# Four weight matrices split once and kept on chip, and eight products in place of nine for each projected chunk

## The reference

```
# layer 0 (layer 1 has the same shape, without the semantic term, and text = first 77 tokens)
q       = heads(x @ W_q)                           # 320 x 320 projection
k_t,v_t = heads(text @ W_k), heads(text @ W_v)     # text = all but the last 4 tokens
probs   = softmax(q @ k_t.T * scale)
qsem    = l2norm(probs @ text)
fused   = q @ k_ip.T * scale + 0.5 * qsem @ l2norm(ip).T
ip_out  = (softmax(fused) * mask) @ v_ip
out     = (probs @ v_t + ip_out) @ W_out + b_out + x   # 320 x 320 projection
```

## Time and profile before

| | |
|---|---|
| median of three runs | 3471.9 us (3469.57 to 3473.32) |
| the profiled execution | 3471.23 us, its span 3469.4 us |
| PE busy | 3351.1 us, 97% of the span |
| DVE busy | 2052.6 us, 59% |
| ACT busy | 1848.9 us, 53% |
| POOL busy | 1095.4 us, 32% |
| granted TensorE clock, mean | 0.990 |

### The profile page before, as it was taken

One profiled execution on the slowest core, in us unless ns is written; L12 is line 12 of the kernel. 1 busy time (PEld: TensorE's weight loads), 2 busy tenths in 40 slices (PEclk: granted clock), 3 DMA queues, 4 the chain that ended last, 5 costly groups with the idle time before them and its releaser, 6 DMA issues.

```text
span 3469.4 us, 65897 instructions
## 1 busy us (share of the span) xinstructions
PE 3351.1 (97%) x24832; PEld 2909.0 (84%) x24832; DVE 2052.6 (59%) x5573; ACT 1848.9 (53%) x4030; POOL 1095.4 (32%) x932
## 2 busy tenths in 40 slices
PE   6999999999999999999999999999999999999868
PEld 4888978887888888888888888888888898889755
DVE  4444455556555565665666556665666656556677
ACT  2333334556555555555655556555655556565757
POOL 2111010234332333233333332333423322222457
PEclk8999999999999999999999999999999999999989
DMA  6433932233358333243356423333336522222232
GB/s 186 112 74 65 106 87 71 71 94 79 89 81 76 94 76 84 78 106 83 96 77 75 93 72 83 81 81 96 99 69 83 68 60 57 61 49 58 52 84 56
DMA packets 659087, 282.78 MB, mean 82 GB/s; under 512 B 481010, under 2 KB 609730, under 8 KB 658772
## 3 DMA queue, kind: packets, MB, share of 16 engines
q1 hardware_dynamic: 658772, 278.57, 38.5%
HBM read 199.44 MB, written 79.04 MB: 80 GB/s over the span
## 4 chain that ended last, share of the span: by engine, by line
PE 87%; DVE 6%; ACT 2%; issue 2%; POOL 1%; DMA 1%; SPq 1%; POOLq 0%; DVEq 0%; ACTq 0%
PE acc L1109 9%; PE acc L1102 9%; PE acc L1105 8%; PE acc L1104 8%; PE acc L1110 8%; PE acc L1103 7%; PE score L1153 4%; PE score L1069 4%; PE spare L1153 4%; PE score L1071 3%; PE av L1140 3%; PE av L1144 3%; PE spare L1192 2%; PE score L1192 2%; PE score L1241 2%
## 5 line engine op out<-in xcount | busy, mean ns | idle before, releaser
L1316 ACT ACTIVATE prob<-score 128x512 f32<-128x512 f32 x1219 | 729.2, 598 | 1205.8 <-PE score L1071 1200.6
L1720 POOL TENSOR_TENSOR prob_lo<-prob,prob_hi 128x512 fp32r<-128x512 f32 x624 | 814.9, 1310 | 1502.1 <-ACT prob_hi L1319 1501.5
L1102 PE MATMUL acc<-tok_v,prob_hi 128*128 128x300 f32 x2240 | 908.8, 406 | 0.9 <-issue 0.9
L1104 PE MATMUL acc<-tok_lo,prob_hi 128*128 128x256 f32 (+1 forms) x2560 | 755.9, 295 | 0.0
L1109 PE MATMUL acc<-tok_v,prob_lo 128*128 128x278 f32 (+1 forms) x2560 | 746.0, 291 | 1.0 <-DVE prob_lo L1424 1.0
L1319 ACT ACTIVATE prob_hi<-score 128x512 fp32r<-128x512 f32 x1219 | 726.1, 596 | 0.0
L1105 PE MATMUL acc<-tok_lo,prob_hi 128*128 128x256 f32 (+1 forms) x2560 | 719.3, 281 | 0.0
L1110 PE MATMUL acc<-tok_v,prob_lo 128*128 128x256 f32 (+1 forms) x2560 | 717.9, 280 | 0.0
L1103 PE MATMUL acc<-tok_v,prob_hi 128*128 128x256 f32 x2240 | 627.7, 280 | 0.0
L1105 PEld LDWEIGHTS acc<-tok_lo,prob_hi 128*128 128x128 f32 (+1 forms) x2560 | 483.8, 189 | 7.2 <-issue 1.8
L1104 PEld LDWEIGHTS acc<-tok_lo,prob_hi 128*128 128x128 f32 (+1 forms) x2560 | 484.5, 189 | 3.6 <-issue 1.9
(11 more groups left out here) (333 smaller groups left out, 5147.6 us busy)
## 6 DMA issues: line engine op xcount, KB each, us to landing
k_ring<-k_scr SPq DMA_DIRECT2D x160, 384.0 KB
tok_v<-v_scr SPq DMA_DIRECT2D x158, 176.0 KB, 3.4
v_ring<-v_scr SPq DMA_DIRECT2D x160, 148.5 KB, 3.4
ctx_t<-in_ctxT SPq DMA_DIRECT2D x16, 1024.0 KB, 8.6
q_ring<-q_scr SPq DMA_DIRECT2D x160, 96.0 KB
v_scr<-v_stage SPq DMA_DIRECT2D x32, 440.0 KB, 2.7
v_scr<-v_stage SPq DMA_DIRECT2D x36, 330.0 KB, 9.5
tok_stage<-in_ctx SPq DMA_DIRECT2D x32, 256.0 KB, 3.1
```

The source lines that it names most:

```text
L1102: e.matmul(out_a[:, 0:SEG + VCOLS], p_hi, tok_v[0:kk, c, seg, v_lo:v_lo + SEG + VCOLS], start=first, stop=False)
L1104: e.matmul(out_a[:, t0:t0 + SEG], p_hi, tok_lo[0:kk, c, seg * SEG:(seg + 1) * SEG], start=False, stop=False)
L1316: e.activation(prob[:, es, :], bank_s[:, :], ACT.Exp, scale=SCALE)
L1720: e.tensor_tensor(prob_lo[:, ps, :], prob[:, es, :], prob_hi.bitcast(F32)[:, ps, :], ALU.subtract).then_inc(s_low[1], 1)
```

## The change

All four matrices are loaded and split once. wq0 is split at the start, and a new job of side "w" with deadline window 12 loads and splits wo0, wq1 and wo1, one after the other. Each has a tile of five blocks of 320 columns: blocks 0, 1 and 4 are the high parts of the three chunks (HI_TILE), 2 and 3 the low parts of chunks 0 and 1 (LO_TILE). The low part of chunk 2 is in the other 64 rows of block 4. The high part of x_in, and of o_t in the closing, stands in both halves of its third chunk, so one product of block 4 with it gives high x high and low x high at once. Products per output chunk are 3 + 3 + 2 = 8.

Each x split has a third ACT copy, and each closing an ACT copy of the high part from one half to the other, which waits for DVE's cast; the products of "finish" on chunk 2 wait for it. The separate staging tiles w_q_raw, w_o_raw and x_raw go: the weights are staged in attn and closing, x in x_res. The low parts of x_in and o_t still have a zeroed half, the other memsets go. Layer-0 jobs have Pause(2) between load and split of x, where they had Pause(1).

The diff, cut to its core:

```diff
+HI_TILE, LO_TILE = (0, 1, 4), (2, 3)
+WEIGHTS = ("wq0", "wo0", "wq1", "wo1")
...
         if UNITS[u][0] == 0:
-            return [w_loads, x_loads, Pause(1), w_split, x_split, Pause(1)] + q
+            return [x_loads, Pause(2), x_split, Pause(1)] + q
         first, second = close(u - B)
-        return [w_loads] + first + [w_split] + second + [lambda: None, x_split, Pause(1)] + q
+        return first + second + [lambda: None, x_split, Pause(1)] + q
+
+    def weights(name):
+
+        def loads():
+            o.add("w_loads", name)
+
+        def split():
+            o.add("w_split", name)
+            put_off(*[("w_split_lo", name, i) for i in range(2)])
+        return [loads, Pause(2), split, drain]
...
-        tasks = [w_split]
+        tasks = [drain]
...
-        return [w_loads] + (fusing if layer == 0 else []) + [Pause(1)], tasks
+        return (fusing if layer == 0 else []) + [Pause(1)], tasks
...
-        if m == 0:
-            o.add("wo_loads", LAST)
...
-        if m == 0:
-            close(LAST)[1][0]()
...
+    add_job([t for name in WEIGHTS[1:] for t in weights(name)], 12, "w")
...
+        w_raw = [attn[:].rearrange("p s h d -> p (s h d)").rearrange("p (k n) -> p k n", k=NM - 1), closing[:, 0:D]]
...
+            def products_of(k):
+
+                if k < NM - 1:
+                    return (HI_TILE[k], 0), (LO_TILE[k], 0), (HI_TILE[k], 1)
+                return (HI_TILE[k], 0), (HI_TILE[k], 1)
...
-                    for i, (wj, xj) in enumerate(((0, 0), (1, 0), (0, 1))):
...
+                    for wj, xj in products_of(k):
+                        mm = e.matmul(bank[bank_of["q", u, m]][0:w, 0:SQ], w_q[:, wj, P * m:P * m + w], x_in[xj][:, k, :],
+                                      start=(wj, xj) == (0, 0), stop=k == NM - 1 and xj == 1)
...
+                    if k == NM - 1 and m == 0:
+                        e.wait_ge(s_turned_twice, turn_nth[u, NM - 1] // NM + 1)
...
+                elif kind == "w_split":
+                    parts, rows = w_parts[s[1]], shared_rows(s[1])[0]
+                    e.wait_ge(s_w, 16 * NM * (w_nth[s[1]] + 1))
+                    e.activation(parts[:, 0:NM - 1, :], w_raw[0], ACT.Copy).then_inc(s_whi, 1)
+                    e.activation(parts[rows, HI_TILE[-1], :], w_raw[1][rows, :], ACT.Copy).then_inc(s_whi, 1)
...
+                    for hi, raw in zip(x_pieces(x_in[0]), x_pieces(x_res)):
+                        e.activation(hi, raw, ACT.Copy).then_inc(s_xhi, 1)
+                    e.activation(x_in[0][high_rows, NM - 1, :], x_res[low_rows, NM - 1, :], ACT.Copy).then_inc(s_xhi, 1)
+                elif kind == "turn" and s[2:] == (NM - 1, ST if UNITS[s[1]][0] == 0 else 0):
+                    e.wait_ge(s_turned, turn_nth[s[1:3]] + 1)
+                    e.activation(o_t[0][low_rows, NM - 1, :], o_t[0].bitcast(F32)[high_rows, NM - 1, :], ACT.Copy).then_inc(s_turned_twice, 1)
...
+                    if x_split_done[s]:
+                        e.wait_ge(s_xhi, 3 * x_split_done[s])
+                        e.wait_ge(s_xlo, 2 * x_split_done[s])
                     for m in range(NM):
-                        e.dma_start(x_raw[0:MW[m], m, :], src[P * m:P * m + MW[m], :]).then_inc(s_x, 16)
+                        if note[s][m]:
+                            e.wait_ge(s_xout[m], 16 * note[s][m])
+                        e.dma_start(x_res[0:MW[m], m, :], src[P * m:P * m + MW[m], :]).then_inc(s_x, 16)
```

More of the change, by code:

```diff
@@ L136, in plan @@
     later, urgent, topq, bgq, current = deque(), deque(), deque(), deque(), []
-    done = dict(part=[0, 0], splits=0, vst=0, xout=[0] * NM, ctx=-1, x_in=-1, wo=-1, w=-1)
+    done = dict(part=[0, 0], splits=0, vst=0, xout=[0] * NM, ctx=-1, x_in=-1, w=-1)
     pieces, slot_no = deque(), [0]
@@ L171, in project_q @@
     def project_q(u):
[L172 to L178, removed]
         def x_loads():
@@ L1290, in _ @@
                             e.wait_ge(*out_of_psum[job["turn", u, NM - 1]])
-                        e.wait_ge(s_lo["wo"], 2 * wo_nth[u] + 2)
+                        e.wait_ge(s_wlo, 2 * w_nth[f"wo{layer}"] + 2)
                         if u == 0:
-                            e.wait_ge(s_pad, 8)
+                            e.wait_ge(s_pad, 2)
                         bank_free(*key)
-                    for i, (wj, oj) in enumerate(((0, 0), (1, 0), (0, 1))):
-                        mm = e.matmul(bank[bank_of[key]][0:w, 0:SQ], w_o[wj][:, k, P * m:P * m + w], o_t[oj][:, k, :],
-                                      start=k == 0 and i == 0, stop=k == NM - 1 and i == 2)
+                    if k == NM - 1 and m == 0:
+                        e.wait_ge(s_turned_twice, turn_nth[u, NM - 1] // NM + 1)
+                    for wj, oj in products_of(k):
+                        mm = e.matmul(bank[bank_of[key]][0:w, 0:SQ], w_parts[f"wo{layer}"][:, wj, P * m:P * m + w], o_t[oj][:, k, :],
+                                      start=(wj, oj) == (0, 0), stop=k == NM - 1 and oj == 1)
                     if k == NM - 1:
@@ L1338, in _ @@
                         sq_count += 1
-                elif kind in SPLITS:
-                    name, raw, (hi, lo), nth_of = SPLITS[kind]
+                elif kind == "w_split":
[3 more added lines that the diff above has]
+                    e.activation(parts[rows, HI_TILE[-1], :], w_raw[1][rows, :], ACT.Copy).then_inc(s_whi, 1)
+                elif kind == "x_split":
                     u = s[1]
-                    if name == "x" and UNITS[u][0] == 1:
-                        raw = x_res
+                    if UNITS[u][0] == 1:
                         e.wait_ge(*out_of_psum[job["finish", u - B, NM - 1]])
                     else:
-                        e.wait_ge(LOADED[name], 16 * NM * ((unit_nth if name == "x" else nth_of)[u] + 1))
+                        e.wait_ge(s_x, 16 * NM * (unit_nth[u] + 1))
                     if note[s] >= 0:
                         e.wait_ge(s_bg, note[s] + 1)
-                    for h, f in zip(rows_of_chunks(name, hi), rows_of_chunks(name, raw)):
-                        e.activation(h, f, ACT.Copy).then_inc(s_hi[name], 1)
+                    for hi, raw in zip(x_pieces(x_in[0]), x_pieces(x_res)):
[4 more added lines that the diff above has]
+                    e.activation(o_t[0][low_rows, NM - 1, :], o_t[0].bitcast(F32)[high_rows, NM - 1, :], ACT.Copy).then_inc(s_turned_twice, 1)
                 elif kind == "max_rows":
@@ L1395, in _ @@
         def _(e):
-            for x in (*w_q, *x_in):
-                e.memset(x.bitcast(F32)[high_rows, NM - 1, :], 0.0).then_inc(s_pad, 1)
-            for x in (*w_o, *o_t):
-                e.memset(x.bitcast(F32)[low_rows, NM - 1, :], 0.0).then_inc(s_pad, 1)
+            for x, rows in ((x_in[1], high_rows), (o_t[1], low_rows)):
+                e.memset(x.bitcast(F32)[rows, NM - 1, :], 0.0).then_inc(s_pad, 1)
             for s in o.steps:
```

83 lines of the change are left out of this document (39 added, 44 removed).

## The result

The kernel after takes 3437.3 us (median of 4 runs, 3435.5 to 3439.0), the kernel before 3472.6 beside it: ratio 0.9898, 95% interval 0.9886 to 0.9910. The sign was right and the size was not.

The account below looks back on a forecast made before the run. TensorE, busy 97% of the span, was taken as the bound. Products 12.2 us plus late weight splits 2.7 made 14.9 off, from the median 3471.9 to 3457.0; its own range was 3452 to 3463, the full range 3447 to 3468.

Parts of the forecast that it names:

- The products: Projection products, nine to eight, 96 fewer: 9.8 us off from 100 to 3280 us, 2.0 after, 0.4 before; 12.2 together.
- The splits in the tail: From 3280 us on, three repeated weight splits stand before TensorE waits of 5.4 us; half taken, 2.7 us off.
- The splits in the middle: From 100 to 3280 us, removed DVE and ACT weight splits: gain between 0 and about 10 us, counted as 0.
- Rival 1: Whole planned order: fewer tasks shift later ones, stalls grow by an eighth, 10.7 us, giving 3467.7; chance 0.18.
- Added copies: Third ACT copy per x split and ACT copy of o_t's third chunk, 16 times each: hidden, 0 us.
- loads: SyncE's queue: 84 of 96 weight DMAs go, but TensorE's longest waits are for ACT and DVE; counted as 0.
- Rival 3: After each turn of the third chunk, the o_t copy holds ACT 2.4 us, 16 times: slower, 3495; chance 0.05.
- Rival 4: From 3280 us on, TensorE's mean clock falls from 0.90 to 0.85, adding 14.5 us: 3471.5; chance 0.03.
- Rival 5: Projection products: eight take as long as nine because weight loads set the spacing, 3469; chance 0.02.
- Rival 2: All 5.4 us of stalls after 3280 us and half the earlier 9.6 us of exponential waits go: 3449.5; chance 0.12.
- What would show it: Expected trace signs: DVE less by about 45 us, ACT by some 21, TensorE waits after 100 us still near 41.

Follow-up runs that it names:

- e1: Kernel before with eight products for nine and the two added ACT copies; order, loads and repeated splits kept: 3464.9 us, ratio 0.9966.
- e2: Kernel after with empty tasks where the old weight work stood, so nearly all steps come in the old order: 3453.7 us, ratio 0.9936.
- e10: Kernel before put in the new order, with eight products and added copies, weights still loaded and split every unit: 3457.0 us, ratio 0.9959.
- e9: Kernel before with all its work, weight loads and splits done inside neighbouring tasks so other steps follow the new order: 3464.7 us, ratio 0.9976.
- e12: e1 without the two added ACT copies and the waits for them: 3462.1 us, ratio 0.9971.
- e18: e17 with ACT's repeated weight copies also cut to one column, the loads kept: 3441.2 us, ratio 0.9895.
- e3: Kernel after with a ninth product, against a tile of zeros, put back on the third chunk: 3450.1 us, ratio 0.9926.
- e13: e10 with DVE's repeated weight subtractions cut to one column, waits and signals kept: 3451.2 us, ratio 0.9936.
- e17: e13 with those one-column subtractions replaced by one-input maxima at the same places: 3447.5 us, ratio 0.9913.

## Why the prediction was right in sign and 20 us off

- **The products, 12.2 us.** 96 are gone, with 344 and 312 in the middle as forecast. Measured 6, 12 and 10 us in three pairs, mean 9. The term is right within the measurement, at its lower side. The earlier trace rows gave 0.12 us each; 9 us over 96 is 0.09. Its division is not borne out: forecast were 10 us up to the tail and 2 in it; by the marks of single executions the pairs gave 2.8, 4.5 and 11.1 us up to the mark and 6.0, 3.8 and 3.9 behind it. That the sum fits is in part luck.
- **The splits in the tail, half of 5.4 us.** This step failed. From e1 to e2 the stretch behind the mark shortened by 7.9, from e10 to the kernel after by 6.9. I had taken the three waits of the earlier trace rows as upper bound and halved it, since "another chain stands close behind each". No such chain held the gain back: it lies above the whole bound. The bound also left out the fall of the clock behind the 3.10 us wait; behind the wait at the same place in e10 it took 1.8 us.
- **The splits in the middle, "neither engine is the bound, and I count nothing".** In the old order that was so: e1 and e2 reach the mark within 0.3 us of each other. In the new order this step failed, by most of 14 us (e10 3249.9, after 3235.7): the mean share of 59% for DVE hid that a row maximum waits behind whatever stands in front of it in DVE's queue. The prediction's own "between 0 and about 10 us" named these waits; taking the lower end gave the wrong value.
- **The order.** Rival 1 was priced as a loss only, though its text said that "it may as well go down". This step failed too. The time went down: 8 us by e9, and 13 from e2 to the kernel after, where the repeated splits are gone. A term that can have either sign should have been a width on both sides of the forecast; then 3447 would not have been the low end.
- **Added copies, loads.** 0 each, borne out by e12 and by e18. Rival 3 is out: no stall of 16 times 2.4 us. Rival 4 too: the clock of the tail went up, 0.90 to 0.92. Rival 5 is out by e3. Rival 2, stalls going in the tail and the middle, was nearest in kind and in time (3449.5), but it took its 5 us from the waits for exponentials, which grew; those for row maxima fell.
- **What would show it.** DVE fell by 58.5 us where 45 were forecast, ACT by 16.3 (21). "PE's waits in the middle still near 41 us" was wrong: 34.0.

The sum by measured pieces, along one path of the table: order 8, products 6, splits 21 (DVE's share 8 for its size and 1 to 8 for its two-input form, ACT's copies 5 or 6), 35 together. Along the other path it is 12, 10 and 13. Not settled is why the two orders differ, by 8 us with the old work and 13 with the new: gaps and the granted clock differ, but no rule was found for which order has fewer gaps; the count of doubled slots, the only one tried, fell.

## What to carry to other kernels

An engine at 59% may still hold up one at 97% where both sit in an in-order chain: price removed work on it by the waits that name it, with the whole of them as the upper end, and add what the clock loses behind a long wait (1.8 us behind one of 3.0 us here). When a change takes tasks out of a planned order, give the new order a term of both signs; here 8 to 13 us of 3472. And look for two-input VectorE instructions beside runs of GpSimd: one of them was held 3.87 us though it was cut to a single column, and 0.14 us with one input. Making all the repeated ones smaller was still worth 8 us in e13, most of it ahead of the tail.

## What the runs showed of the hardware

A VectorE subtraction of 64x1 elements beside a run of GpSimd subtractions took 3.87 us (e13), a maximum of 64x2 at the same place 0.14 (e17); the 64x320 subtraction took 3.32 both before and in e10. The rule that the Trainium skill has (SBUF — State Buffer, "Who interferes with whom") is that the two engines share one pair of ports by an exclusive lock, taken by VectorE for two SBUF inputs or in its faster modes, and that reductions never contend. The runs agree: in none of the traces of this case does a VectorE reduction take over 0.70 us, beside GpSimd or not. That page says, of the faster modes, that whoever comes second is blocked for the whole of the other's instruction. Most stretched subtractions of these traces fit one instruction: no other takes over 2 us, and the 1.22 us one of e17 got in between two of GpSimd's run. At this one place, and in every kernel that has this split with two inputs, it was held up to the end of GpSimd's run, through the rest of one instruction and two or three more, 3.3 to 3.9 us in all. What decides between the two is not shown.

Nor is one input always enough. Two casts of the same form in the kernel after, the second while GpSimd worked from 3343.11 to 3345.61:

```profile
3342.11 0.29 DVE L1444 CAST part_bf<-part_f 64x256 bf16<-64x256 f32 x1
...
3343.11 2.50 POOL L1731 TENSOR_TENSOR prob_lo<-prob,prob_hi 128x512 fp32r<-128x512 f32 x2
...
3344.18 1.58 DVE L1449 CAST part_bf<-part_f 64x256 bf16<-64x256 f32 x1
```

The cast took 1.58 us instead of 0.29 and ended at 3345.76, just behind GpSimd.
